# Second mixer of a six-stage decoder: gate columns in the kept experts' order, and no expert map per token

## The reference, cut to what matters

```python
logits = x @ gate_weight.T                       # 2048 x 128 old experts
logits = jnp.where(old_to_new[None, :] == -1, -jnp.inf, logits)
probs = jax.nn.softmax(logits, axis=-1)
top_v, top_i = jax.lax.top_k(probs, TOP_K)       # TOP_K = 8
top_v = top_v / jnp.sum(top_v, axis=-1, keepdims=True)
sel_new = old_to_new[top_i]                      # new number, 0 to 47
oh = (flat_e[:, None] == jnp.arange(E)[None, :])
pos = jnp.sum(jnp.cumsum(oh, axis=0) * oh, axis=-1) - 1
valid = pos < CAP                                # CAP = 192
```

## Time and profile before

| | us |
|---|---|
| median of 3 runs | 2162.82 (2157.24 to 2168.64) |
| the profiled execution, its own time | 2158.87 |
| its span | 2157.1 |
| busy: PE / DVE / POOL / ACT | 1739.3 / 1523.6 / 1086.7 / 956.8 |
| second mixer, batches 0 to 3 and drain | about 1178 to 1706 |
| last scatter into the table issued | 1718.73 |
| mean granted clock of TensorE | 0.891 of full |

### The profile page before, as it was taken

One profiled execution on the slowest core, in us unless ns is written; L12 is line 12 of the kernel. 1 busy time (PEld: TensorE's weight loads), 2 busy tenths in 40 slices (PEclk: granted clock), 3 DMA queues, 4 the chain that ended last, 5 costly groups with the idle time before them and its releaser, 6 DMA issues. The chain is left out here.

```text
span 2157.1 us, 34592 instructions
## 1 busy us (share of the span) xinstructions
PE 1739.3 (81%) x9155; PEld 1383.7 (64%) x9156; DVE 1523.6 (71%) x2883; ACT 956.8 (44%) x1867; POOL 1086.7 (50%) x817
## 2 busy tenths in 40 slices
PE   4898989347999999999998888788832079999990
PEld 3566565236888888888886555555421078888880
DVE  4477777765777888887884323788879757777774
ACT  4355452312444444444443324444423157777773
POOL 1000624564667667667676000044538657777763
PEclk9899989657999999999999898888865589999995
DMA  8011111035888888888896613131010369999967
GB/s 322 28 40 59 31 48 40 1 122 152 206 208 212 205 227 211 223 228 212 218 231 153 198 21 59 59 59 59 1 59 23 126 194 256 258 250 256 257 149 254
DMA packets 138553, 318.80 MB, mean 148 GB/s; under 512 B 30713, under 2 KB 31321, under 8 KB 136825
## 3 DMA queue, kind: packets, MB, share of 16 engines
q1 hardware_dynamic: 71448, 201.74, 27.1%
q0 software_dynamic: 64752, 112.04, 26.8%
q10 hardware_dynamic: 2288, 4.29, 0.5%
HBM read 238.68 MB, written 97.62 MB: 156 GB/s over the span
## 5 line engine op out<-in xcount | busy, mean ns | idle before, releaser
L98 POOL DMA_INDIRECT tab_rows<-pair,slot x256 | 313.7, 1226 | 452.6 <-DVEq L752 296.6
L90 PE MATMUL gu<-wgu_h,xgT_h 128*128 x648 | 233.5, 360 | 7.3 <-DVE xgT_l L1428 3.7
L1253 POOL DMA_INDIRECT xg<-x_rows,ids x167 | 191.5, 1147 | 62.5 <-issue 48.5
L90 PE MATMUL gu<-wgu_l,xgT_h 128*128 x648 | 219.6, 339 | 0.0
L90 PE MATMUL gu<-wgu_h,xgT_l 128*128 x648 | 218.3, 337 | 0.0
L1308 ACT ACTIVATE ysb<-yp,wts 128x512 f32<-128x512 f32 x160 | 110.1, 688 | 144.7 <-PE yp L1535 144.7
L90 PE MATMUL guk<-xgT_hk,wgu_hk 128*128 128x192 f32 x576 | 161.7, 281 | 0.0
L90 PE MATMUL guk<-xgT_lk,wgu_hk 128*128 128x192 f32 x576 | 158.8, 276 | 0.0
L90 PE MATMUL guk<-xgT_hk,wgu_lk 128*128 128x192 f32 x576 | 158.8, 276 | 0.0
L1298 ACT ACTIVATE sg<-gu 128x192 f32<-128x192 f32 x162 | 53.6, 331 | 235.1 <-PE gu L90 235.1
L1428 DVE TENSOR_TENSOR xgT_l<-tpx,xgT_h 128x512 fp32r<-128x512 f32 x163 | 112.2, 688 | 55.6 <-ACT xgT_h L1294 53.4
(11 more groups left out here) (503 smaller groups left out, 5043.3 us busy)
## 6 DMA issues: line engine op xcount, KB each, us to landing
wgu_sb<-in_wgu SPq DMA_DIRECT2D x64, 768.0 KB
wgu_sbk<-in_wgu SPq DMA_DIRECT2D x48, 768.0 KB, 4.4
wd_sb<-in_wd SPq DMA_DIRECT2D x64, 256.0 KB
wd_sbk<-in_wd SPq DMA_DIRECT2D x48, 256.0 KB, 5.3
ct<-in_ctxT SPq DMA_DIRECT2D x8, 1024.0 KB, 5.0
wd_sb<-in_wd SPq DMA_DIRECT2D x64, 128.0 KB
wd_sbk<-in_wd SPq DMA_DIRECT2D x48, 128.0 KB, 5.8
odd_rows<-zero SPq DMA_DIRECT2D x1, 4352.0 KB, 15.5
```

Of the source, the lines that this page charges most:

```text
L90: i = nc.tensor.matmul(out, left(k), right(k), start=(start and k == 0 and m == 0), stop=(k == ops - 1 and m == 2))
L98: nc.gpsimd.indirect_dma_start(out=tab, out_offset=bass.IndirectOffsetOnAxis(ap=s["slot"][:, n:n + 1].bitcast(U32), axis=0), in_=s["pair"] ...
L1253: nc.gpsimd.indirect_dma_start(out=xg[:, t % G, :], out_offset=None, in_=x, in_offset=bass.IndirectOffsetOnAxis(ap=ids[:, t:t + 1].bitcast ...
```

## The change

The gate is now loaded as it is stored, old expert by hidden, with one old expert on each partition, and the map as one number a partition. VectorE makes `onto`, a 128 x 48 one-hot (old by new), in fp32 and bf16. TensorE multiplies each 128-wide piece of the gate by it (`gate_in_new_order`), which leaves the gate columns in the order of the new experts in PSUM, and a product of ones with the bf16 copy tells which new experts exist. VectorE copies both out. The logits then have 48 columns, and the index that FIND_INDEX8 gives is the new number. The one-hot over 128, the product with the map, the halving adds, the reduction and the test for a negative number are gone; `iota16` and `o2nx` with them. Waits on `s_set` (7 to 6) and `s_dset` follow.

```diff
-            for dst, src in ((wo, "wo1"), (gate, "gate1")):
+            for dst, src in ((wo, "wo1"), (gate_old, "gate1")):
...
-            sp.dma_start(o2ni[:, :], d["o2n"].to_broadcast([P, EOLD])).then_inc(s_w, 16)
+            sp.dma_start(o2ni[:, :], d["o2n"]).then_inc(s_w, 16)
...
-            nc.gpsimd.iota(iota16[:, :, :], [[1, EOLD], [0, BT * TOPK]], base=0, channel_multiplier=0,
-                           allow_small_or_imprecise_dtypes=True).then_inc(s_set, 1)
...
-                c.done(nc.vector.tensor_copy(e816[:, rows], e8[:, js[0]:js[-1] + 1, :].rearrange("p j k -> p (j k)")))
-                c.wait()
-                nr = nj * TOPK
-                old = hotold[:, :, at:at + nr]
-                c.done(nc.vector.tensor_tensor(old, iota16[:, :, 0:nr], e816[:, rows].unsqueeze(1).to_broadcast([P, EOLD, nr]), ALU.is_equal))
-                c.wait()
-                c.done(nc.vector.tensor_tensor(old, old, o2nx[:, :, 0:nr], ALU.mult))
-                c.wait()
-                src = old
-                with nc.allow_low_precision("one number below 128 and zeros"):
-                    for t in halves:
-                        w = src.shape[1] // 2
-                        c.done(nc.vector.tensor_tensor(t[:, :, at:at + nr], src[:, 0:w, :], src[:, w:2 * w, :], ALU.add))
-                        c.wait()
-                        src = t[:, :, at:at + nr]
-                c.done(nc.vector.tensor_reduce(en[:, rows], src.rearrange("p e n -> p n e"), AX.X, ALU.add))
-                c.wait()
-                c.done(nc.vector.tensor_copy(en16[:, rows], en[:, rows]))
+                for t in (en16, en):
+                    c.done(nc.vector.tensor_copy(t[:, rows], e8[:, js[0]:js[-1] + 1, :].rearrange("p j k -> p (j k)")))
                 c.wait()
...
-                c.done(nc.vector.scalar_tensor_tensor(ok[:, rows], en[:, rows], 0.0, ok[:, rows], ALU.is_ge, ALU.mult))
...
-            split_xT(0)
             dve.wait_ge(s_w, 16 * NW)
             nc.vector.tensor_copy(o2n[:, :], o2ni[:, :]).then_inc(s_dset, 1)
             dve.wait_ge(s_dset, KC + 4)
-            nc.vector.tensor_copy(o2nx[:, :, :], o2n[:, :].unsqueeze(2).to_broadcast([P, EOLD, BT * TOPK])).then_inc(s_dset, 1)
-
-            nc.vector.tensor_scalar(gone[:, :], o2n[:, :], -1.0, -1e30, ALU.is_equal, ALU.mult).then_inc(s_dset, 1)
+            for t in (onto, onto16):
+                nc.vector.tensor_scalar(t[:, :], iotax[:, :, 0], o2n[:, 0:1], None, ALU.is_equal).then_inc(s_dset, 1)
+            split_xT(0)
...
+                    dve.wait_ge(s_fold, KC + 2)
+                    nc.vector.tensor_copy(gate[:, :, :], tb[:, 0, 0:KC * E1].rearrange("p (k e) -> p k e", e=E1)).then_inc(s_dset, 1)
+                    nc.vector.tensor_scalar(gone[:, :], tb[:, 0, KC * E1:(KC + 1) * E1], 0.0, -1e30, ALU.is_equal, ALU.mult).then_inc(s_dset, 1)
...
+            def gate_in_new_order():
+
+                pe.wait_ge(s_dset, KC + 6)
+                for kc in range(KC):
+                    nc.tensor.matmul(tb[:, 0, kc * E1:(kc + 1) * E1], gate_old[:, kc * P:(kc + 1) * P], onto[:, :], start=True, stop=True)
+                nc.tensor.matmul(tb[:, 0, KC * E1:(KC + 1) * E1], s["ones"][:, :], onto16[:, :], start=True, stop=True).then_inc(s_fold, 1)
...
                     pe.wait_ge(s_dset, KC + 3)
+                    gate_in_new_order()
                     queries(a, range(KC))
```

More of the change, by code:

```diff
@@ L1883, in mixer_two @@
         rr = sb("rr", [P, BT])
-        gate = sb("gate1", [P, KC, EOLD])
+        gate = sb("gate1", [P, KC, E1])
         bqkv, dec, bon = (s[n] for n in ("bqkv", "dec", "bon"))
-        o2n16 = sb("o2n16", [P, EOLD], BF16)
-        iota16 = sb("iota16", [P, EOLD, BT * TOPK], BF16)
-        o2nx = sb("o2nx", [P, EOLD, BT * TOPK], BF16)
         iotax = sb("iotax", [P, E1, BT * TOPK], BF16)
-        gone = sb("gone", [P, EOLD])
+        gone = sb("gone", [P, E1])
         empty = sb("empty3", [P, E1 * REG1 // P + 1, 2], I32)
@@ L1914, in mixer_two @@
         zero, bout = kk[:, 0, :], v[:, 0, :]
-        o2n, o2ni = ee[:, 0, 0:EOLD], ee[:, 1, 0:EOLD].bitcast(I32)
+        onto, o2n, o2ni, gate_old = ee[:, 0, 0:E1], ee[:, 1, 0:1], ee[:, 1, 1:2].bitcast(I32), ee[:, 2, :]
+        onto16 = ee[:, 3, 0:E1 // 2].bitcast(BF16)
         x5, x5T = aa, ee
-        hotold = a2[:, :, :].rearrange("p k n -> p (k n)").bitcast(BF16)[:, 0:BT * TOPK * EOLD].rearrange("p (e n) -> p e n", n=BT * TOPK)
         hot = a2[:, :, :].rearrange("p k n -> p (k n)").bitcast(BF16)[:, 0:BT * TOPK * E1].rearrange("p (e n) -> p e n", n=BT * TOPK)
-        halves = [e2[:, :, :].rearrange("p k n -> p (k n)").bitcast(BF16)[:, lo:lo + BT * TOPK * w].rearrange("p (e n) -> p e n", e=w)
-                  for lo, w in ((0, EOLD // 2), (BT * TOPK * EOLD // 2, EOLD // 4), (0, EOLD // 8))]
         where = e2[:, :, :].rearrange("p k n -> p (k n)")[:, 0:BT * TOPK * E1].rearrange("p (e n) -> p e n", n=BT * TOPK)
         wqT, wkT, wvT, wo = a2, e2, aa, p1[:, :, 1:S + 1]
-        lg = e2[:, :, :].rearrange("p k n -> p (k n)")[:, BT * TOPK * E1:].rearrange("p (j e) -> p j e", e=EOLD)
+        lg = e2[:, :, :].rearrange("p k n -> p (k n)")[:, BT * TOPK * E1:BT * TOPK * E1 + BT * E1].rearrange("p (j e) -> p j e", e=E1)
         v8 = sb("v83", [P, BT, TOPK])
@@ L1995, in mixer_two @@
         DN3, DR3 = done2[2] + (B - 1) * N2, 2 * (B - 1) + BT
-        KRT, KSL = 20, 17
+        KRT, KSL = 14, 16
         @block.sync
@@ L2090, in _ @@
         def _(act):
-            act.wait_ge(s_set, 7)
+            act.wait_ge(s_set, 6)
             def folded(done, ic, bank, at, scale):
@@ L2236, in _ @@
             dve.sem_inc(s_idx, 1)
-            dve.wait_ge(s_set, 7)
+            dve.wait_ge(s_set, 6)
             def norm1(n, peeled):
@@ L2361, in norm3, with route_rows @@
                 assert c.n == N2, c.n
-            def route_rows(c, js, logits, at):
+            def route_rows(c, js, logits):
                 rows = slice(js[0] * TOPK, (js[-1] + 1) * TOPK)
                 nj = len(js)
-                c.done(nc.vector.tensor_tensor(lg[:, js[0]:js[-1] + 1, :], logits, gone[:, :].unsqueeze(1).to_broadcast([P, nj, EOLD]), ALU.add))
+                c.done(nc.vector.tensor_tensor(lg[:, js[0]:js[-1] + 1, :], logits, gone[:, :].unsqueeze(1).to_broadcast([P, nj, E1]), ALU.add))
                 c.wait()
@@ L2448, in route @@
                 dve.wait_ge(s_lg, b + (ROUTED + 1))
-                yield from route_rows(c, range(BT), lgp, 0)
+                yield from route_rows(c, range(BT), lgp)
                 assert c.n == KRT, c.n
@@ L2496, in route_j @@
                     dve.wait_ge(s_lg, (B - 1) + (ROUTED + j + 1))
-                    for _ in route_rows(c, range(j, j + 1), mm[:, j:j + 1, 0:EOLD], (BT - 1) * TOPK):
+                    for _ in route_rows(c, range(j, j + 1), mm[:, j:j + 1, 0:E1]):
                         pass
@@ L2661, in output_folded @@
                     i.then_inc(s_fold, 1)
-                pe.wait_ge(s_dset, 2 * KC + 11)
+                pe.wait_ge(s_dset, 2 * KC + 13)
             def drained(b):
@@ L2676, in logits @@
                     for kc in range(KC):
-                        i = nc.tensor.matmul(mm[:, j, 0:EOLD], x5T[:, kc, j * P:(j + 1) * P], gate[:, kc, :],
+                        i = nc.tensor.matmul(mm[:, j, 0:E1], x5T[:, kc, j * P:(j + 1) * P], gate[:, kc, :],
                                              start=(kc == 0), stop=(kc == KC - 1))
```

29 lines of the change are left out of this document (14 added, 15 removed).

## The result

| | before | after |
|---|---|---|
| median (runs) | 2161.89 us (2157.05 to 2168.64, 6) | 2147.23 us (2144.5 to 2153.88, 6) |
| ratio, 95% interval | | 0.9933 [0.9913, 0.9952] |
| profiled execution, its own time (span) | 2158.87 (2157.1) | 2148.72 (2147.0) |
| mean granted clock | 0.891 | 0.887 |

A forecast was written before the change was run, and what follows sets the result against it. Bounds: TensorE's way to positions in batches 0 and 1, VectorE's mask in batch 2, GpSimd's scatters in the drain. Gains 0.35 + 9.45 + 3.2 = 13.0, less 1.7 for clock: 11.3 us, giving 2151.5 us; range 2142 to 2161.

The forecast's parts named there:

- Batch 2, 9.45 us: Second mixer, batch 2: TensorE idles for VectorE's mask, so the whole saving between logits and mask shortens the path, 9.45 us.
- Batches 0 and 1 worth nothing on VectorE: Second mixer: VectorE's 9.27 us saved per batch only lengthens its wait for positions, to about 15 us; 0.35 left in all.
- Setup covered: Before the first query product: new VectorE steps, gate products and map load hide in existing waits; 0 us, bounds -0.9 and +0.5.
- rival of a late map: Setup: map loaded as 128 small pieces lands late, VectorE and queries wait; kernel slower, 2170 if landing takes 40 us; 4%.
- The clock, 1.7 us: Batch 0: logits begun at low clock stay low with 48 columns, costing 3.4 us; half subtracted because a low start is uncertain.
- A stage that begins high loses nothing: Logits stages: those starting at a high granted clock keep it with 48 columns, so no time is lost, 0 us.
- rival of a clock lost in several stages: Batches 0 and 1, or all three, lose clock; gain only 6.2 or 2.9 us, time 2156.6 to 2160; 12%.
- Width for TensorE: Logits on TensorE: width hardly counts below 128 columns; 48 columns save 0.07 us a batch, bounds 0.05 and 0.2.
- Drain, 3.2 us: Batch 3's drain: VectorE's first tile comes earlier, GpSimd's gap before its scatters shrinks from 3.50 to 0.30, gaining 3.2 us.
- GpSimd's gap stays: Rival for the drain: the gap is GpSimd's own, not from VectorE's tile; gain 8.1 us, time 2154.7; 7%.
- The other three tiles: Drain, tiles after the first: VectorE at 6 us a tile hides behind GpSimd's 10.3; gain nothing, otherwise 9.9 us.
- My own sign of being wrong: Stage after the mixer: a change in its length by more than 1 us would show the forecast wrong.

The follow-up runs named there:

- pad_b2: Changed kernel plus a VectorE reduction of about 8.3 us where the map stood, in batch 2 only; ratio to the kernel before 1.0006.
- pad_loop: Changed kernel plus a VectorE reduction of about 8.3 us where the map stood, in batches 0 and 1 only; ratio to the kernel before 0.9941.
- logits_64: Changed kernel with batch logits 64 columns wide, gate padded with zero columns; one run, logits to positions 29.0, 24.1 and 9.3 us in batches 0, 1, 2.
- before_again: Kernel before the change, unedited, profiled again beside the experiments; one run, 531.4 us from the first query to the first gather.
- after_again: Changed kernel, unedited, run again beside the experiments; ratio to the kernel before 0.9971.
- before_hold: Kernel before the change, with weight loads from the third expert on held until the finished table is loaded; ratio to the kernel before 0.9978.
- late_end: Changed kernel plus one VectorE reduction of about 12 us at the end of the last batch's drain; ratio to the kernel before 1.0013.
- pad_drain: Changed kernel plus a VectorE reduction of about 3.1 us in each of the drain's last three tiles; ratio to the kernel before 0.9980.
- pos_early: Changed kernel with TensorE making the drain's first tile's positions ahead of the last two tiles' logits; ratio to the kernel before 0.9959.

## Why the prediction was right, and where it wasn't

- **Batch 2, 9.45 us: right.** 9.26 measured from logits add to positions; 0.4 us went to the clock in the logits themselves. pad_b2 gives it back.
- **Batches 0 and 1 worth nothing on VectorE: right.** pad_loop shows it. The wait became 17.8 and 17.4 us, not 15, as TensorE got slower.
- **Setup covered: right.** The map landed 9.5 us after its issue. The rival of a late map is refuted.
- **The clock, 1.7 us: too small, and the reason partly wrong.** The step that failed is "A stage that begins high loses nothing". I drew it from the 64-column logits of the first mixer and carried it over to 48. For 64 columns it holds (logits_64, batch 1); with 48 the logits of batches 0 and 1 began high and fell: 1.68 + 3.25 = 4.9 us. "Begun low, the stretch stays low" was right: in the four profiles with 48 columns in which batch 0's clock fell at once, the batch took 29.0 us in place of 25.8, 3.2 us where I had 3.4. My rival of a clock lost in several stages was the truer case, though in the profiled pair by a fall inside the stage and not by a low start.
- **Width for TensorE: right.** At half clock eight products take 1.78 us with 48 columns and 1.91 with 128; narrow logits are not narrow. The Trainium skill ("TensorE: Matmul & The Clock Gate", LDWEIGHTS) lets the time of a weight load go by the 128 columns of the stationary side, and the trace agrees. The 60 cycles for up to 64 columns in its section Back-to-back issue gap are not seen here; the section gives them for an isolated product, so it does not speak against itself, as I had it.
- **Drain, 3.2 us: wrong, 0 measured.** The failed step is "GpSimd's gap can shrink from 3.50 to the usual 0.30"; it is 4.19. I took VectorE's first tile as its chain of instructions and did not ask when TensorE would have the positions if the mask came 3.3 us sooner. The earlier trace rows stand before and behind this wait, which was 0.37 us. TensorE's order of four tiles ahead was visible in the code, and its logits ended only 2.17 us before the positions, so at the old pace the order alone would have taken back 1.1 us (3.3 - 2.17, an estimate). The other 2.8 us are the clock again, which stayed at 0.50 in the drain's logits, and for which I had no term there. The rival "GpSimd's gap stays" gave the right consequence from another cause.
- **The other three tiles "give nothing": wrong.** They let VectorE's block end 11.8 us earlier, and with it SyncE's weight loads, whose wait I had not looked up. That gave 6.3 us between the last scatter and the gather in the first pair, and 1.9 between before_again and after_again. before_hold shows the weight loads as the cause of the slow table, late_end and pad_drain that VectorE's end moves them. My own sign of being wrong, that the stage after the mixer changes its length by more than 1 us, came true with 7.6.
- **The sum.** Forecast -11.3; the profiled pair -10.2 = -8.9 (batch 2) + 4.9 (clock in batches 0 and 1) + 0.4 (drain and its way there) - 6.3 - 1.3 (behind the mixer) + 1.0 (setup, up to batch 1, not the change's as far as the profiles show). Two misses of 3.2 us each on one side and one of 7.6 on the other nearly cancel: batch 2 was foreseen, but that the total fits is luck. The 1.3 us behind the first gather have no cause shown.

## What to carry to other kernels

When an engine gets faster up to a wait, look up what the releasing engine has queued ahead of the answer, at its new earlier time. When an engine becomes free earlier behind the bound, list what starts with its end (a block's barrier, a prefetch) and what that meets in the DMA queues: here this was worth 6.3 us in one pair of profiles, beside 8.9 for the path itself, and 1.9 in another. When moving such a load out of the way, look what it meets at its new time. Before narrowing the moving side of small products, compare the clock in the stretch behind them: at full clock 128 columns took 3.84 us where 64 took 3.79, so padding with zero columns is cheap here, and it kept the clock in batch 1. Whether it pays in the time of the whole kernel isn't settled.

## What was not expected of the hardware

- Busy TensorE can lose its clock. In batch 1 it stands busy 2.00 of every 2.00 us from 1498 on and the granted clock is 0.50 from 1500 to 1506, after two waits of 0.93 and 0.67 us; with 128 columns it stays at 1.00. The Trainium skill ("TensorE: Matmul & The Clock Gate", What's actually happening) has the fall follow idleness; in this stretch the trace shows none, and what else brought the fall stays open.
- One small load, of the finished table (96 KB), takes 1.9 to 5.9 us, by and large by how far ahead the weight loads were issued. By lead: 21.4 us, 1.9; 17.6, 3.2; 16.9, 3.4; 16.8, 3.8; 16.2, 3.1; 15.1, 4.0; 13.3, 5.2; 12.3, 5.7; 12.1, 5.9; 11.2, 4.7; 10.9, 5.7; 10.6, 5.9.
- In the experiments' profiles the drain has waits that no data explains (TensorE 2.55 us "issue" in pos_early, 6.54 in before_again; VectorE 4.74 us "remote" in pos_early), and GpSimd's gap is 8.5 to 9.7 us in place of 4, in both kernels (5.8 to 6.1 with early positions). In each of these twelve profiles TensorE's stall overlaps the 5 to 6 us in which SyncE's copies to x_rows and acc_rows keep the DMA engines' busy share at about 1, and it ends with them or up to 1.6 us later. The first pair has the same copies without the stall, so what these engines wait for stays open.
